# A conv-recurrence, attention and expert kernel: bias products over 128 rows, logits with tokens on partitions, and the skip taken by DVE in the recurrence

## The reference

```python
# layer 0: x is (16, 96, 16, 16)
h_in = shuffle(conv(x, w_i2s * mask))             # 192 gate channels, 1x3
for row in rows:                                  # 16 steps
    s = conv1d(h, w_s2s) + h_in[row]
    o, f, i, g = split(sigmoid(s), 4)
    c = f * c + i * g
    h = o * tanh(c)                               # 48 channels
x = x + conv(out_h, w_skip * mask_skip) + b_skip  # 96 channels

# layer 1: t is (16, 256, 96), tokens of an image
t = t + attention(layernorm(t))                   # causal, 6 heads, + bp
u = layernorm(t)
p = softmax(u @ gate_w + gate_b)                  # 4 experts
m = p * top2_mask(p); m = m / (sum(m) + 1e-9)
y = sum_e m[e] * (gelu(u @ w1[e] + b1[e]) @ w2[e] + b2[e])
out = t + y
```

## Time and profile before

| what | value |
|---|---|
| median of 3 runs | 453.63 us (453.16 to 453.68) |
| the profiled execution | 454.55 us |
| its span, first to last instruction | 452.7 us |
| mean granted clock of TensorE | 0.985 of full speed |
| PE busy | 426.3 us, 94% |
| PEld / DVE / ACT / POOL busy | 345.8 / 257.5 / 265.2 / 161.0 us |
| chain that ended last | PE 70%, DVE 11% |

### The profile page before, as it was taken

The page is one execution under the profiler, slowest core; times in us unless marked ns, Lnnn a source line. Parts: engine busy times, 40 slices in busy tenths (PEclk is TensorE's granted clock), DMA queues, the critical chain, the costliest instruction groups (busy, mean ns, idle before and its releaser), DMA issues.

```text
span 452.7 us, 10725 instructions
## 1 busy us (share of the span) xinstructions
PE 426.3 (94%) x3186; PEld 345.8 (76%) x3186; DVE 257.5 (57%) x856; ACT 265.2 (59%) x741; POOL 161.0 (36%) x343
## 2 busy tenths in 40 slices
PE   4999998878899999999999999999999999999897
PEld 4999997446568877877787788778877887787676
DVE  2677777466525862686177537743863585267424
ACT  2444554266566648664865585567657764866370
POOL 5122112445432542362256314631542254236100
PEclk9999999967999999999999999999999999999999
DMA  8700000130021002101210120022002100200000
GB/s 177 166 0 0 0 0 1 29 77 20 0 59 30 20 8 72 45 1 36 54 32 0 45 54 23 0 54 51 17 0 61 43 0 19 68 19 2 19 1 17
DMA packets 16472, 14.94 MB, mean 33 GB/s; under 512 B 7586, under 2 KB 13588, under 8 KB 16452
## 3 DMA queue, kind: packets, MB, share of 16 engines
q1 hardware_dynamic: 14788, 13.87, 12.3%
q10 hardware_dynamic: 1472, 0.68, 0.6%
q0 software_dynamic: 192, 0.15, 0.2%
HBM read 3.86 MB, written 1.57 MB: 12 GB/s over the span
## 4 chain that ended last, share of the span: by engine, by line
PE 70%; DVE 11%; issue 7%; POOL 4%; ACT 4%; DMA 2%; SPq 1%; DVEq 1%; POOLq 0%; ACTq 0%
PE F L1071 18%; PE T L1029 7%; PE A L1050 6%; PE F L1087 4%; PE F L1091 4%; PE S L1013 4%; PE F L1088 4%; PE S L1015 3%; POOL p_sb L436 3%; PE F L1067 3%; DVE fc L691 2%; PE S L1018 2%; DVE cell L693 2%; ACT tc_sb L520 2%; PE F L910 2%
## 5 line engine op out<-in xcount | busy, mean ns | idle before, releaser
L436 POOL TENSOR_SCALAR p_sb<-p_sb,rden 128x128 f32<-128x128 f32 (+1 forms) x192 | 79.2, 427 | 127.0 <-DVE rden L755 124.9
L1071 PE MATMUL F<-w_sb,hid 128*128 128x96 f32 x768 | 101.0, 276 | 0.0
L1071 PEld LDWEIGHTS F<-w_sb,hid 128*128 128x128 f32 x768 | 93.4, 192 | 6.0 <-issue 6.0
L581 ACT ACTIVATE p_sb<-S,nmax 128x128 f32<-128x128 f32 (+1 forms) x192 | 78.7, 423 | 13.3 <-DVE nmax L749 12.7
L749 DVE TENSOR_REDUCE nmax<-S 128x2 f32<-128x512 f32 (+1 forms) x80 | 50.6, 633 | 48.1 <-PE S L1018 48.0
L498 ACT COPY pt_sb<-T 128x512 f32<-128x512 f32 (+1 forms) x48 | 26.4, 550 | 51.9 <-PE T L1029 51.9
L1029 PE MATMUL T<-id_sb,p_sb 128*128 128x128 f32 x288 | 48.7, 288 | 7.8 <-POOL p_sb L436 7.2
L627 ACT ACTIVATE hid<-F,b_sb 128x512 f32<-128x512 f32 x72 | 49.3, 686 | 8.2 <-PE F L1091 7.6
L1029 PEld LDWEIGHTS T<-id_sb,p_sb 128*128 128x128 f32 x288 | 32.0, 146 | 17.9 <-POOL p_sb L436 12.5
L1013 PE MATMUL S<-k_bd,q_st 96*128 96x384 f32 (+2 forms) x96 | 39.8, 422 | 3.1 <-DMA k_bd<-k_cur 3.0
L581 ACT ACTIVATION_READ_ACCUMULATOR p_sb<-S,nmax 128x1 f32 x192 | 39.7, 207 | 0.0
(11 more groups left out here) (144 smaller groups left out, 798.5 us busy)
## 6 DMA issues: line engine op xcount, KB each, us to landing
k_bd<-k_cur SPq DMA_DIRECT2D x93, 32.0 KB, 2.0
q_st<-q_cur SPq DMA_DIRECT2D x28, 96.0 KB, 2.2
k_bd<-k_cur SPq DMA_DIRECT2D x93, 16.0 KB, 1.8
t_st<-t_cm SPq DMA_DIRECT2D x7, 192.0 KB, 2.4
out_y<-y_sb SPq DMA_DIRECT2D x7, 192.0 KB, 1.9
x_pad<-in_x SPq DMA_DIRECT2D x2, 612.0 KB, 7.8
w_sb<-in_w SPq DMA_DIRECT2D x1, 576.0 KB
hid<-in_w SPq DMA_DIRECT2D x1, 576.0 KB, 7.6
```

What stands on the lines that cost most here:

```text
L436: last = nc.gpsimd.tensor_scalar(p, p, rden[:, u % 3, i:i + 1], 1.0, ALU.mult, ALU.mult)
L581: last = nc.scalar.activation(p_sb[:, u % 3, i * nk:(i + 1) * nk], S[u % 2][:, i * nk:(i + 1) * nk], ACT.Exp, bias=nmax[:, u % 3, i:i + 1] ...
L1071: last = mm(dst[:, e * C:(e + 1) * C], hid[:, c, s * TT:(s + 1) * TT], w2_sb[:, c], start=False, stop=(c == NCH - 1), skip_group_check=True)
```

## The change

1. The skip in the recurrence. `take_skip` of ACT and `add_input` of POOL are gone. DVE's new `add_skip` reads the product in PSUM, adds bias and input row in one instruction and writes `t_cm`. It stands between `new_cell` and `new_h`, for the half-step two before. PE's `skip` now waits for `t_half`.
2. `ones2` and `b2hl` have 128 rows in place of 2. The 126 others are zeros, set by two memsets on POOL at the start.
3. The logits. `route_logits` multiplies, tile by tile, the normalized tokens as stationary operand by the 4 columns of the gate's weights: 12 weight loads of 128 columns and 12 products of 4 columns, straight to tokens on partitions. The copy to `gt_sb` and the transposes are gone.

```diff
-        b2hl = sb("b2hl", [2, E * C], F32R)
-        ones2 = sb("ones2", [2, 128], F32R)
+        b2hl = sb("b2hl", [128, E * C], F32R)
+        ones2 = sb("ones2", [128, 128], F32R)
...
+            nc.gpsimd.memset(as_f32(ones2[:]), 0.0).then_inc(zeroed, 1)
+            nc.gpsimd.memset(as_f32(b2hl[:]), 0.0).then_inc(zeroed, 1)
...
-            def add_input(m, hb, row):
-
-                pool.wait_ge(skip_taken, m + 1)
-                dst = skip_out(row, hb)
-                nc.gpsimd.tensor_tensor(dst, dst, x_row(row)[:, hb * HALF:(hb + 1) * HALF, 1:], ALU.add
-                                        ).then_inc(t_half, 1)
...
-            def take_skip(m, hb, row):
-
-                act.wait_ge(skip_ready, m + 1)
-                nc.scalar.activation(skip_out(row, hb), K[hb][0:C, 0:HC].rearrange("p (b w) -> p b w", w=W), ACT.Identity,
-                                     bias=bsk_sb[:, 0:1]).then_inc(skip_taken, 1)
...
-                    if c == 3:
-                        act.wait_ge(route_ready, n + 1)
-                        nc.scalar.copy(gt_sb[:], M[0:E, :]).then_inc(route_copied, 1)
...
+            def add_skip(m, hb, row):
+
+                dve.wait_ge(skip_ready, m + 1)
+                V.scalar_tensor_tensor(skip_out(row, hb), K[hb][0:C, 0:HC].rearrange("p (b w) -> p b w", w=W),
+                                       bsk_sb[:, 0:1], x_row(row)[:, hb * HALF:(hb + 1) * HALF, 1:], ALU.add, ALU.add
+                                       ).then_inc(t_half, 1)
...
-            with dve.Fori(1, ROWS) as row:
+            with dve.Fori(2, ROWS) as row:
                 for hb in range(2):
                     new_cell(2 * row + hb, hb)
+                    add_skip(2 * row - 2 + hb, hb, row - 1)
                     new_h(2 * row + hb, hb)
...
-                    pe.wait_ge(skip_taken, m - 1)
+                    pe.wait_ge(t_half, m - 1)
...
+            def route_logits(n):
+
+                for s in range(SPB):
+                    ts = slice(s * TT, (s + 1) * TT)
+                    last = split3(M[:, s * E:(s + 1) * E], x2hi[:, ts], x2lo[:, ts], whi[:, 2 * C:2 * C + E],
+                                  wlo[:, 2 * C:2 * C + E], skip_group_check=True)
+                last.then_inc(route_t_ready, 1)
...
-                split3(M[:], whi[:, 2 * C:], wlo[:, 2 * C:], x2hi[:], x2lo[:]).then_inc(route_ready, 1)
-                expert_hidden(n, range(3, 6), first)
-                wait_alone(pe, route_copied, n + 1)
-                for s in range(SPB):
-                    ins = nc.tensor.transpose(M[:, s * E:(s + 1) * E], gt_sb[:, s * TT:(s + 1) * TT], id_sb[0:E, 0:E])
-                ins.then_inc(route_t_ready, 1)
-                expert_hidden(n, range(6, 9), first)
+                route_logits(n)
+                expert_hidden(n, range(3, 9), first)
```

More of the change, by code:

```diff
@@ L153, in hybrid_kernel @@
         x2lo = sb("x2lo", [C, BT], F32R)
-        gt_sb = sb("gt_sb", [E, BT])
         gl = sb("gl", [128, SPB, E])
@@ L201, in hybrid_kernel @@
         x2t_ready = sem("x2t_ready")
-        route_ready = sem("route_ready")
         route_t_ready = sem("route_t_ready")
@@ L215, in hybrid_kernel @@
         x2hi_done = sem("x2hi_done")
-        route_copied = sem("route_copied")
         route_exp = sem("route_exp")
@@ L220, in hybrid_kernel @@
         h_ready = sem("h_ready")
-        skip_taken = sem("skip_taken")
         t_half = sem("t_half")
@@ L261, in hybrid_kernel @@
         N_WIN = 14
+        N_ZEROED = 7
         N_WREC = 6
@@ L280, in wait_alone @@
                 value = eng.snap(eng.to_reg(value))
-            eng.wait_ge(zeroed, 5)
+            eng.wait_ge(zeroed, N_ZEROED)
             eng.wait_ge(semaphore, value)
@@ L383, in body @@
                     stage(n + 2)
-            sp.wait_ge(zeroed, 5)
+            sp.wait_ge(zeroed, N_ZEROED)
             sp.wait_ge(t_half, STEPS)
@@ L407, in _ @@
             nc.gpsimd.memset(nhalf[:], -0.5).then_inc(zeroed, 1)
-            pool.wait_ge(zeroed, 5)
+            nc.gpsimd.memset(as_f32(ones2[:]), 0.0).then_inc(zeroed, 1)
+            nc.gpsimd.memset(as_f32(b2hl[:]), 0.0).then_inc(zeroed, 1)
+            pool.wait_ge(zeroed, N_ZEROED)
             def rstd1(n):
@@ L520, in cell_out @@
                 nc.scalar.activation(tc_sb[UP, hb], cell[UP, hb], ACT.Tanh).then_inc(cell_tanh, 1)
-            def take_skip(m, hb, row):
-                act.wait_ge(skip_ready, m + 1)
-                nc.scalar.activation(skip_out(row, hb), K[hb][0:C, 0:HC].rearrange("p (b w) -> p b w", w=W), ACT.Identity,
-                                     bias=bsk_sb[:, 0:1]).then_inc(skip_taken, 1)
[L528 to L539, removed]
+            for q in range(4):
+                cell_gates(q, q % 2, G[q])
+                cell_out(q, q % 2)
             with act.Fori(1, ROWS // 2) as it:
                 for q in range(4):
-                    half_step(4 * it + q, q, 2 * it + q // 2)
-            for hb in range(2):
-                take_skip(STEPS - 2 + hb, hb, ROWS - 1)
+                    cell_gates(4 * it + q, q % 2, G[q])
+                    cell_out(4 * it + q, q % 2)
             act.wait_ge(w_in, 16 * N_WIN)
@@ L676, in split_expert_weights @@
             def split_expert_weights():
-                setup_step(V.memset(as_f32(ones2[:]), 1.0))
+                dve.wait_ge(zeroed, N_ZEROED)
+                setup_step(V.memset(as_f32(ones2[0:2]), 1.0))
                 dve.wait_ge(w_act, 2)
@@ L683, in split_expert_weights @@
                 dve.wait_ge(w_dve, W_ALL - 1)
-                setup_step(V.scalar_tensor_tensor(b2hl[:], b2l[:], id_sb[0:2, 1:2], b2p[:], ALU.mult, ALU.add))
+                setup_step(V.scalar_tensor_tensor(b2hl[0:2], b2l[:], id_sb[0:2, 1:2], b2p[:], ALU.mult, ALU.add))
                 assert steps[0] == W_ALL
@@ L704, in new_h @@
                 V.tensor_tensor(h_pad[UP, bs, 0:W], o, t, ALU.mult).then_inc(h_ready, 1)
+            def add_skip(m, hb, row):
[3 more added lines that the diff above has]
+                                       ).then_inc(t_half, 1)
+            dve.wait_ge(x_in[0], 16)
             for m in range(2):
@@ L708, in _ @@
                 new_h(m, m, first=True)
-            with dve.Fori(1, ROWS) as row:
+            for hb in range(2):
+                new_cell(2 + hb, hb)
+                add_skip(hb, hb, 0)
+                new_h(2 + hb, hb)
+            for i in (1, 2, 3):
+                dve.wait_ge(x_in[i], 16)
+            with dve.Fori(2, ROWS) as row:
                 for hb in range(2):
                     new_cell(2 * row + hb, hb)
+                    add_skip(2 * row - 2 + hb, hb, row - 1)
                     new_h(2 * row + hb, hb)
+            for hb in range(2):
+                add_skip(STEPS - 2 + hb, hb, ROWS - 1)
             split_qk_weights()
```

## The result

The changed kernel takes 441.25 us (median of 4 runs, 439.67 to 441.85); the kernel before, timed beside it, 453.65 us (453.16 to 454.31). The ratio is 0.972, 95% interval 0.9692 to 0.9749: 12.4 us faster. Forecast were 440.2 us and a range of 437.0 to 447.2.

What follows compares the result with a forecast made beforehand. Bounds: DVE in the recurrence, nearly tied with PE after the change; PE in the blocks and closing products. Sum: -4.9 (skip) - 9.1 (bias products) + 0.6 (logits) = -13.4, so 453.63 becomes 440.2 us; range 437 to 447.2.

Steps and rivals of the forecast that it cites:

- 28 x 0.15 = 4.2 us: Recurrence: 28 half-steps after the fill each fall from 2.15 to 2.00 us with the skip on DVE; bounds 2.0 to 5.1.
- or still 0.46 where that was it: Recurrence, from L693's end to the h product: 0.41 us with the new instruction, or an unchanged 0.46; mean 0.435.
- The end of the recurrence, 0.7 us: From the last skip product to the transposes: they start at 79.50 instead of 80.18 us, 0.7 us gained.
- Each bias product at full height 0.37 us cheaper: Bias products: 0.55 us each falls to 0.18 with 128 rows; bounds 0 and 0.37, the upper taken.
- B: Rival: bias products are dear through operand type (fp32r), not rows, so part 2 gives 0; 449.3 us, chance 0.12.
- Per middle block 0.37 + 0.37 + 0.29 + 0.06: Savings of a middle block's four bias products that arrive: 1.09 us per block, 7.6 us over 7 blocks.
- that copy leads through DVE and POOL to PE's wait at 247.43: 0.29: Middle block, third bias product: its saving meets DVE, busy except for 0.29 us up to the copy, so 0.29 arrives.
- +0.08 per block: Logits: 12 loads at 0.11 us, 1.32 us, replace 1.24 us of PE; +0.6 us for eight blocks.
- D: Rival: each short logit product takes load and passage one after the other, 0.39 us a pair; slower, 467.6 us, chance 0.03.
- The clock, counted as nothing: First block's start-up at lower clock moves forward whole, 0 us; a third's change in the low stretch would be 2.6 us.
- C: Rival: in the blocks the softmax chain over DVE, ACT and POOL takes part 2's saving back; 446.8 us, chance 0.12.
- E: Rival: DVE gets worse in the recurrence, half-steps 2.15 us or more, only the end's 0.7 gained; 444.4 us, chance 0.05.

Runs made afterwards that it cites:

- noadd_pool_idle: Kernel before without POOL's add of the input row in the recurrence, nothing added to DVE; 448.26 us, ratio 0.988.
- rows64: Changed kernel with ones2 and b2hl over 64 rows in place of 128; 450.56 us, ratio 0.9931 to the kernel before.
- rows96: Changed kernel with ones2 and b2hl over 96 rows in place of 128; 441.40 us, ratio 0.9733 to the kernel before.
- p2_bias_only: Kernel before with only the bias products over 128 rows (ones2, b2hl and their two memsets); 447.57 us, ratio 0.9868.
- xh_8_columns: Changed kernel normalizing only 8 of the 96 columns of xh from block 1 on; 438.05 us, ratio 0.9673 to the kernel before.
- late_bias_2rows: Changed kernel with each block's third and fourth bias products back at 2 rows, the closing ones left at 128; 442.12 us, ratio 0.9738 to the kernel before.
- p3_logits_only: Kernel before with only the new logits, tokens on partitions, in place of the three products and transposes; 454.45 us, ratio 1.0021.
- p1_skip_only: Kernel before with only the skip taken by DVE (add_skip in place of take_skip and add_input); 448.10 us, ratio 0.9873.

## Why the prediction was right, point by point

Timed, 12.4 us were gained and 13.4 forecast. In the profiled executions the first step of the recurrence that the change can touch (the third h product) stood at 15.24 us against 15.62 before; over all fourteen traces it stood between 14.62 and 15.86, so 0.4 of the 12.8 us of span are no gain. 12.4 remain.

- **Half-steps, "28 x 0.15 = 4.2 us".** Right in its mechanism, small by 0.7 us. From the third h product to the last there are 29 half-steps; they took 62.35 us before and 57.48 after, 4.9 us. The new instruction was forecast at 0.35 us and took 0.347. What was off is "or still 0.46 where that was it": no half-step waits for tanh any more, DVE sets the step at 1.98 us in nearly all of them, and 29 half-steps gained where 28 were counted. That DVE's long operations were POOL's doing is shown by noadd_pool_idle.
- **The end of the recurrence, 0.7 us.** Measured 1.55 - 0.90 = 0.65.
- **Each bias product at full height 0.37 us cheaper.** Shown by the closing tiles (1.4 us for four) and by rows64 and rows96. The choice of the upper bound, by the likeness to the 4 x 4 transposes, was right in its outcome; no run tried those transposes. B falls.
- **"Per middle block 0.37 + 0.37 + 0.29 + 0.06".** The first two held, and the fourth's 0.06 was nearly right (0.00): part 2 alone gives 0.78 us per block, and L1140 waits as forecast. The step that failed is the third, "that copy leads through DVE and POOL to PE's wait at 247.43: 0.29". That path exists, but another wait comes first: between the product and 247.43 PE passes the transposes of xh (L979, now L965), and DVE's row up to xh starts from exponentials, not from the product. The loads there now wait 0.35 us, and xh_8_columns shows that this row sets the pace: 0.14 us out of it, 0.16 off the pace. The third product gave 0.00 in the middle blocks, together with the fourth (late_bias_2rows: 0.01). 6 x 0.29 = 1.7 us of the sum were lost here; the wait of 0.61 us for POOL stayed as it was.
- **The last body** gained 1.70 us where 1.0 was forecast: there all four products count (0.40 for the late two), 0.08 belongs to the closing ones (above), and p3_logits_only has it 0.12 shorter, not longer. 0.32 of it comes with part 1 alone (41.52 to 41.20), nearly all at one place: PE's last wait for POOL's scaling is 0.76 us before (at 417.75) and 0.46 in p1_skip_only (at 411.15), because a gap on DVE ahead of it is gone (last section).
- **Part 3, "+0.08 per block".** The pitch of 0.11 us held; p3_logits_only has +0.11 per block, and 0.9 us timed where 0.6 was forecast. D falls: it would have taken a pitch of 0.25.
- **The clock, counted as nothing.** The low stretch stayed in the first body, but it was shorter: summed over stretches of 4 us from 80 to 132 us, 13.6 us at the lower level before and 10.2 after. The first bodies follow it over the fourteen traces: 49.7 to 49.95 us where it lasted about 13.6, 49.2 to 49.3 with 10.2, 48.2 to 48.3 with 6.9, and 47.4 to 48.0 with 3.4. So the first body's gain goes with the shorter low stretch, and no run shows that the change brought that about. The allowance of 2.6 us was of the right size, and the four runs of the changed kernel go the same way, from 441.85 at a mean clock of 0.987 to 439.67 at 0.996.
- **Rivals.** C was a quarter right: its chain takes back part of the middle blocks' saving, 0.3 of 1.1 us, not all. E falls: the half-steps took 1.98 us.

So the sum came within 1.1 us of the time by errors that partly cancel, and that part is luck. Too little was forecast for the half-steps (0.7), for the first body (0.5, the clock) and for the last (0.7); too much for the six middle bodies (2.1: 1.7 for the third product, the rest for the fourth and part 3), for the closing products (0.2, of which 0.08 stands in the last body's row), and by a delay that wasn't foreseen (0.4, below).

## What to carry to other kernels

A product with 64 rows or fewer between products of full height cost much more here than its columns say. Pad it with zero rows (96 were enough) and count what the neighbours lose, not what its own row shows. Work taken from GpSimd can speed up another engine more than it costs it: look for operations of one form with two durations, and see what the other engine does in the longer ones. When a saving on the bounding engine is followed forward, stop at the first instruction that waits for another engine whose row doesn't begin with the saved work: the saving ends there, whatever a later wait would have given.

## What was not expected of the hardware

- The price of a product's height is a step: 64 rows cost as much as 2 (tile 3.22 us), 96 as little as 128 (2.86).
- A DVE operation on 8 columns is hardly shorter than on 96: four of them (L713) took 1.06 against 1.20 us.
- Behind the recurrence DVE stood 0.5 us before its own next operation, for which nothing was missing that the trace shows. The changed kernel, timeline of DVE:

```profile
75.38 0.74 DVE L704 BATCH_NORM_STATS2 st<-t 128x6 f32<-128x96 f32 x4 [0.76 <-ACT t L523]
76.65 0.38 DVE L707 BATCH_NORM_AGGREGATE mv<-st 128x2 f32<-128x6 f32 x4 [0.53 <-DVE st L704]
```

  Before, the second followed at once (82.01 to 82.11). It is the 0.42 us lost ahead of block 0. But the kernel before has such a gap too, elsewhere, in its last body:

```profile
415.45 0.18 DVE L766 BATCH_NORM_AGGREGATE mv<-st 128x2 f32<-128x6 f32 x1 [0.48 <-DVE st L764]
```

  All fourteen traces have exactly one between these two operations. The ten kernels with `add_skip` on DVE have it behind the recurrence (0.52 or 0.53 us); the four without it (before, p2_bias_only, p3_logits_only, noadd_pool_idle) have it in the last body (0.48). So the gap moved, and cost 0.42 us at one end and gave 0.3 back at the other. It goes with DVE's own program, which `add_skip` made longer, so fetching its instructions may be the reason; that is argued, and no run here shows it.
- Executions differ by up to 1.2 us in when the recurrence gets under way (third h product at 14.62 to 15.86), and by up to 2.5 us in the first body (47.42 to 49.95 us), the latter with the length of the low-clock stretch. The code in these stretches is the same or nearly so.
